# A macaron block of two feed-forwards and a retention layer on one core: the third feed-forward by seven block products of W2 instead of eight, with the block sums of W2 built one feed-forward earlier

## The reference

```
x = x + 0.5 * ffn(layernorm(x))
x = x + attention(layernorm(x))
x = x + 0.5 * ffn(layernorm(x))

ffn(h)       = fwht(silu(h W1^T) * (h W3^T)) W2^T      # W1, W3: 2048 x 512, W2: 512 x 2048
attention(h) = chunked linear attention with per-head decay, 16 heads of 32, 4 chunks of 128,
               ternary-quantised qkv and output weights, RMS norms in front and behind
```

## Time and profile before

| | us |
|---|---|
| median of 3 runs | 2299.95 (2299.61 to 2300.54) |
| profiled execution | 2298.74 |
| its span, first to last instruction | 2297.0 |
| TensorE busy | 2274.4 (99%) |
| VectorE busy | 1518.2 (66%) |
| ScalarE busy | 925.9 (40%) |
| GpSimd busy | 219.4 (10%) |
| share of the 16 DMA engines, main queue | 46.6% |

### The profile page before, as it was taken

How to read it: one execution, slowest core, us unless ns; L and a number is a source line. 1 busy time by engine, 2 the same in 40 slices (tenths; PEclk the granted TensorE clock), 3 DMA queues, 4 the chain that set the end, 5 groups by cost and what they waited for, 6 DMA issues and landing times. The chain is left out here.

```text
span 2297.0 us, 48771 instructions
## 1 busy us (share of the span) xinstructions
PE 2274.4 (99%) x19551; PEld 1775.0 (77%) x19551; DVE 1518.2 (66%) x3430; ACT 925.9 (40%) x1897; POOL 219.4 (10%) x206
## 2 busy tenths in 40 slices
PE   9999999999999999999999999999999999999998
PEld 5444444687888788888888888788878887888887
DVE  7677456676777667767666677676667766666544
ACT  7646134434343433344334344433344344334322
POOL 0290014110000000000000000000010000000000
PEclk9999999999999999999999999999999999999999
DMA  9866533344444533555255345632546326442422
GB/s 243 224 160 180 161 100 86 121 121 126 130 118 127 147 92 119 134 140 139 74 154 140 91 129 140 154 93 81 165 118 148 97 77 173 102 118 78 117 92 67
DMA packets 349698, 291.57 MB, mean 127 GB/s; under 512 B 253600, under 2 KB 278432, under 8 KB 346656
## 3 DMA queue, kind: packets, MB, share of 16 engines
q1 hardware_dynamic: 349040, 287.66, 46.6%
q10 hardware_dynamic: 432, 0.79, 0.1%
HBM read 173.02 MB, written 59.77 MB: 101 GB/s over the span
## 5 line engine op out<-in xcount | busy, mean ns | idle before, releaser
L1960 PE MATMUL d_bank<-w2t,work 128*128 128x256 f16 x2496 | 374.4, 272 | 2.4 <-DMA work<-w_dram 2.4
L1535 DVE SCALAR_TENSOR_TENSOR work<-l_bank,l_scale,work 128x256 f32<-128x256 f32 x416 | 181.7, 478 | 260.6 <-PE l_bank L1928 259.9
L1928 PE MATMUL g_bank<-work,w1t 128*128 128x256 f16 x2688 | 311.7, 272 | 1.8 <-ACT work L1172 1.8
L1928 PE MATMUL l_bank<-work,w3t 128*128 128x256 f16 x2688 | 311.7, 273 | 0.0
L1928 PEld LDWEIGHTS l_bank<-work,w3t 128*128 128x128 f16 x2688 | 261.7, 98 | 36.4
L1928 PEld LDWEIGHTS g_bank<-work,w1t 128*128 128x128 f16 x2688 | 259.9, 98 | 33.9 <-ACT work L1172 2.4
L1552 DVE TENSOR_TENSOR work<-work 128x256 f16<-128x256 f32 (+1 forms) x416 | 257.1, 618 | 33.3 <-ACT work L1184 32.8
L1182 ACT CAST work<-work 128x256 f16<-128x256 f32 x208 | 84.1, 404 | 470.3 <-DVE work L1540 466.4
L1960 PE MATMUL d_bank<-work 128*128 128x256 f16 x1872 | 272.5, 273 | 0.5 <-DVE work L1552 0.5
L1172 ACT ACTIVATE work<-g_bank,g_scale 128x256 f32<-128x256 f32 x416 | 173.6, 468 | 236.5 <-PE g_bank L1928 236.4
L1960 PEld LDWEIGHTS d_bank<-w2t,work 128*128 128x128 f16 x2496 | 240.6, 98 | 35.2 <-issue 2.9
(11 more groups left out here) (282 smaller groups left out, 2915.7 us busy)
## 6 DMA issues: line engine op xcount, KB each, us to landing
work<-w_dram SPq DMA_DIRECT2D x208, 384.0 KB, 3.4
work<-parts_dram SPq DMA_DIRECT2D x192, 128.0 KB, 3.4
x_dram<-work SPq DMA_DIRECT2D x16, 1024.0 KB, 4.6
work<-x_dram SPq DMA_DIRECT2D x24, 512.0 KB, 4.6
parts_dram<-q_parts SPq DMA_DIRECT2D x32, 256.0 KB, 2.1
parts_dram<-k_parts SPq DMA_DIRECT2D x32, 256.0 KB, 2.4
norm_dram<-cent SPq DMA_DIRECT2D x32, 256.0 KB, 2.3
w2t<-in_L_ffn_W_dram SPq DMA_DIRECT2D x31, 256.0 KB, 3.5
```

The lines of the kernel that those rows point to most:

```text
L1535: nc.vector.scalar_tensor_tensor(out=tokens, in0=l_bank[:, HALF * e:HALF * (e + 1)], scalar=l_scale[:, tile:tile + 1], in1=second_gate if ...
L1928: ins = nc.tensor.matmul(dst[:, HALF * e:HALF * (e + 1)], wt[:, wp, k, P * tile:P * (tile + 1)], f.x[:, s_half, xp, k, :], start=(k == 0 a ...
L1960: ins = nc.tensor.matmul(bank_m[:, cols], combos[:, q % 2, hp, combo, :], weights[:, wp, :], start=(p == 0 and opens and hp == wp), stop=( ...
```

## The change

`FAST` becomes 2, so that n = 2 is done by seven block products too; the plain `feed_forward` falls away, and the fast one takes its name. The step `w2sums` is split in two: GpSimd's part keeps the name, the casts, low parts and the store become `w2halve`. Both are now hung on slots: `w2sums` p at slot 3p - 14 (-14, -11, -8, -5, -2, 1, 4, 7), `w2halve` p at slot 3p - 11 (-11, -8, -5, -2, 1, 4, 7, 10). The first four of the `w2halve` steps thus stand among the `down` steps of n = 1, the rest in n = 2. The f32 sums and one single staging buffer `w2_staged` lie in `yt`, the operand of n = 3; ACT waits for the store of pair p - 1 before it writes the staging buffer for p. TensorE waits for the sums pair by pair in the first half of n = 2, and no longer for all of them. The layer norm `("ffn1", 3)` moves from slot 19 to slot 12, since n = 2 now writes x1 half-way.

```diff
-    FAST = 3
+    FAST = 2
...
-        w2_sums = at["hid_f32"].rearrange("p (i d) -> p i d", i=4)
+        w2_sums = at["yt"][:, 0:4 * HALF].rearrange("p (i d) -> p i d", i=4)
+        w2_staged = at["yt"][:, 4 * HALF:7 * HALF].bitcast(F16).rearrange("p (a i d) -> p a i d", a=2, i=3)
...
+            for p in range(PAIRS):
+                add(slots, max(3 * p - 14, -HT), [("w2sums", p)])
+                add(slots, 3 * p - 11, [("w2halve", p)])
...
-            for at, b in ((19, 3), (109, 4), (253, 5), (353, 6), (470, 7)):
+            for at, b in ((12, 3), (109, 4), (253, 5), (353, 6), (470, 7)):
...
-        for n in range(2, FAST):
+        for n in range(FAST, 2 * B):
             STEPS += feed_forward(n, SLOTS)
-        for n in range(FAST, 2 * B):
-            STEPS += fast_feed_forward(n, SLOTS)
...
-                elif step == "w2sums":
+                elif step == "w2halve":
                     sp.wait_ge(w2_sum_lo, 2 * (arg + 1))
-                    sp.dma_start(w2_dram[arg], streamed[:, arg % 2]).then_inc(w2_stored[arg % 2], 16)
+                    sp.dma_start(w2_dram[arg], w2_staged).then_inc(w2_stored[arg % 2], 16)
...
-                elif step == "w2sums":
+                elif step == "w2halve":
                     p = arg
                     act.wait_ge(w2_differences, p + 1)
-                    if p >= 2:
-                        act.wait_ge(w2_stored[p % 2], 16 * (p // 2))
                     nc.scalar.copy(w2t[:, p, 0, HALF:D], w2_sums[:, 0]).then_inc(w2_sum_hi, 1)
-                    nc.scalar.copy(streamed[:, p % 2, 0], w2_sums[:, 1:4]).then_inc(w2_sum_hi, 1)
+                    if p:
+                        act.wait_ge(w2_stored[(p - 1) % 2], 16 * ((p - 1) // 2 + 1))
+                    nc.scalar.copy(w2_staged[:, 0], w2_sums[:, 1:4]).then_inc(w2_sum_hi, 1)
...
                     pe.wait_ge(w2_streamed[q % 2], 16 * (q // 2 + 1))
+                    if n == FAST and s_half == 0:
+                        pe.wait_ge(w2_sum_lo, 2 * (p + 1))
                     if p == 0:
-                        pe.wait_ge(w2_sum_lo, 2 * PAIRS)
                         pe.wait_ge(res_done, TT * FAST)
```

37 lines of the change are left out of this document (7 added, 30 removed).

## The result

| | before | after |
|---|---|---|
| median | 2300.13 (2298.31 to 2301.49, 15 runs) | 2304.74 (2303.25 to 2308.90, 15 runs) |
| ratio to before | | 1.0022, 95% interval 1.0015 to 1.0029 |
| profiled execution | 2298.74 | 2304.92 |
| span | 2297.0 | 2303.2 |
| mean granted clock | 1.000 | 0.997 |

What follows compares the result with a forecast made beforehand. TensorE was taken as the bound, busy for 2274.4 of 2297.0 us. The terms -3.7 - 4.0 + 1.8 + 0.6 + 0.2 summed to -5.1 us, giving a median of 2294.8 us, range 2291.8 to 2299.5.

Steps and rivals of the forecast that it cites:

- Step 1: In n = 2, fewer matmul columns, with pairs of 7.53 us: 3.7 us less.
- Step 2: In n = 2, TensorE's three stalls at 358 to 365 us go: 4.0 us less.
- rival (c): The n = 2 stalls move instead of going, 3 us return: sum -2.1, 2297.8 us; chance 0.13.
- Step 3: In n = 1, reloads come late behind the store of pair 1: 1.8 us more, bounds 0 and 5.
- Rival (a): In n = 1, norm operations collide with GpSimd's adds at the shared port; reloads cost 5.0: 2298.0 us, chance 0.17.
- Step 4: Start of n = 2: added DVE work delays v's second half, 0.6 us more, bounds 0 and 2.2.
- Step 5: Rest of n = 2: more DVE work per pair and sixteen new streams, 0.2 us more, bounds 0 and 2.
- The prediction's own test: The prediction counts as wrong if, among other signs, n = 2 as a whole is not shorter by 6 us or more.
- Rival (d): In n = 1, a store in SP's queue holds up reload 13; 8 us late gives 2302.8 us; chance 0.05.

Runs made afterwards that it cites:

- b_nosums: The kernel before the change, with the building of W2's block sums left out and plain pieces stored instead: 2295.37 us, ratio 0.9980.
- e_norm: The changed kernel with the layer norm of batch 3 at slot 16 instead of 12: 2302.02 us, ratio 1.0009.
- e_comb2: Changed kernel: v before k's transposes, pair 1's store behind reloads, batch 3's norm at 16, n = 2's store at 51, later sums re-slotted: 2295.18 us.
- e_early: The changed kernel with casts and low parts of pairs 0 and 4 to 7, and pair 1's adds, in earlier slots: 2305.89 us, ratio 1.0027.
- e_nosums: The changed kernel with the building of W2's block sums left out and plain pieces stored instead: 2298.27 us, ratio 0.9994.
- e_vfirst: The changed kernel with batch 0's v in front of the transposed k in slot 1: 2301.63 us, ratio 1.0008.
- e_plain_tuned: The changed kernel without W2's block sums, v in front of k's transposes, n = 2's result store at slot 51: 2291.81 us, ratio 0.9965.
- e_store: The changed kernel with only the store of n = 2's result moved to slot 51: 2303.03 us, ratio 1.0014.
- e_filler: The changed kernel with 12 unneeded matmuls of 512 columns in the wait between v's halves: 2305.60 us, ratio 1.0026.

## Why the prediction was wrong

**Step 1, fewer columns, was right.** A pair of n = 2 without attention work takes 424.56 - 417.03 = 7.53 us in the changed kernel:

```profile
417.03 2.78 PE L1904 MATMUL g_bank<-xt,w1t 128*128 128x256 f16 x24
...
424.56 0.67 PE L2009 MATMUL a_bank<-work 128*128 128x128 f16 x9
```

**Step 2 was right on the old stalls and wrong on what is late next.** No wait is left between 340 and 370 us, and `b_nosums` prices the old ones at 4.6 us by the medians and 4.1 by the traces. But a stall of the same kind came at 331 us, which is rival (c). I had ended `w2sums` 7 near 320 us by a period of 8.3 us a pair. (The prediction's own numbers give 265.5 + 6 x 8.3 = 315.3.) It ended at 329.63, because the casts and low parts of pairs 5 to 7 stand at fixed places in DVE's and ACT's order, three slots apart, and DVE reached them at 309.58, 321.08 and 330.95: 10 to 12 us a pair, set by the slots and not by the chain. GpSimd stood idle for 7.7, 7.5 and 5.1 us in front of pairs 5, 6 and 7, waiting for DVE. In size this is the largest miss of the sum: 3.4 us of idle time and 2.9 us of slow matmuls behind it, against 0. `e_norm` and `e_comb2` take the stall away in the two pieces that stood in front of the score, 1.2 us each.

**Step 3 had the right mechanism, and its size was off by 0.9 us.** After the change the chain runs as the prediction has it. First GpSimd's timeline, the adds and differences of `w2sums` 1:

```profile
259.51 3.06 POOL L962 TENSOR_TENSOR work<-w2t 128x512 f32<-128x512 f16 x2 [9.35 <-DVE work L1499]
262.65 1.05 POOL L964 TENSOR_TENSOR work<-work 128x256 f32<-128x256 f32 x1
...
265.72 1.05 POOL L967 TENSOR_TENSOR work<-work 128x256 f32<-128x256 f32 x1
```

DVE beside it, two row operations of the norm and the last low parts of pair 1:

```profile
260.11 1.46 DVE L1649 SCALAR_TENSOR_TENSOR cent<-work,mean,qnw_row 128x512 f32<-128x512 f32 x1
...
263.23 1.03 DVE L1649 SCALAR_TENSOR_TENSOR cent<-work,mean,qnw_row 128x512 f32<-128x512 f32 x1
...
267.98 0.96 DVE L1499 TENSOR_TENSOR work<-work 128x768 f16<-128x768 f32 x1 [0.31 <-ACT work L1135]
```

And SP's queue, the store of pair 1 and the three reloads behind it:

```profile
268.96 0.32 SPq L785 DMA_DIRECT2D w_dram<-work  x1
269.39 1.37 SPq L737 DMA_DIRECT2D work<-hid_dram  x3
```

`w2sums` 1 started at 259.51 (forecast 259.5), took 7.3 us (6.0), and the reloads went out at 269.39 (268.2), where before they went at 264.53. The wait in front of `down` 13 is 1.46 us (1.5); that these two agree is luck, since the reloads went out 1.2 us later than forecast and `down` 13 was itself held back by the wait in front of `down` 11. What I had priced at nothing is the shift of the norm's rows and of the reloads between their transposes: it costs the 0.91 us in front of `down` 11. `e_early`, with pair 0's casts ahead of the norm, has neither wait. Rival (a), by which every norm operation beside the adds collides, stood for a turn of 9.2 us. The Trainium skill, "SBUF — State Buffer", section "Who interferes with whom", states that rule. The trace agrees that there is a collision, in both directions (1.46 and 1.03 us for operations of 0.75, 1.05 for differences of 0.72), but the turn grew by 1.8 us, less than half of the 3.8 that five full collisions would make.

**Step 4 is the step that failed.** It was priced at 0.6 us and cost 2.8 us of idle time and 1.7 us of slow matmuls. I had listed the instructions in front of v's low parts, and then not added their durations. They are in one piece of DVE's timeline:

```profile
289.42 0.88 DVE L1511 SCALAR_TENSOR_TENSOR work<-l_bank,l_scale,work 128x256 f32<-128x256 f32 x2 [3.56 <-PE l_bank L1904]
...
291.26 1.40 DVE L1492 SCALAR_TENSOR_TENSOR work<-d_bank,ffn_unscale,xin 128x512 f32<-128x512 f32 x2
292.58 0.41 DVE L1528 TENSOR_TENSOR work<-work 128x256 f16<-128x256 f32 x1
292.91 0.55 DVE L1707 TENSOR_TENSOR kT<-k_turned_parts 128x384 f32<-128x384 f16 x1
```

Before, the step of `lin` took DVE from 286.44 to 287.11, 0.67 us, and then came the transposed k; now `hlin`, two `resid` and `hlow` take 292.91 - 289.42 = 3.49 us ahead of it. From there to v's low parts, over the transposed k and ACT's cast and copies, it is 2.30 us in both kernels (287.11 to 289.41, and 292.91 to 295.21). The difference, 2.82, is the growth of the wait from 0.29 to 3.13 (2.84). There was no slack to set against it, since TensorE had already waited there before. `e_nosums` shows that the sums have no part in it, `e_vfirst` and `e_plain_tuned` that the order of v and k decides 2.3 us of it.

**Step 5 had the resource right and missed its place.** The streams of n = 2 cost nothing. The one of n = 3 came late by 1.5 us, behind the store of n = 2's result, which is issued 13.8 us after the start of n = 3 where it was 10.3 (455.34 - 441.57, and 444.64 - 434.29); it went with the store (`e_store`).

**A term was missing: the clock.** Nowhere did the sum allow for what follows a stall of 3 us. In the profiled execution it was 1.7 + 1.65 + 1.28 = 4.6 us of the 6.2 us by which the two spans differ; in that of the kernel before the clock never fell. `e_filler` and `e_store` show the part of v without it.

How much of it is in the median can be estimated, since each run's mean granted clock is on record. Of 80 runs of the kernel before, made beside the experiments, the 12 at 1.000 have a median of 2298.1 us, the 53 at 0.999 one of 2299.9 and the 15 at 0.998 one of 2301.4. So the forecast, which took 1.2 us from the profiled execution to the median, took it from an execution without a fall. The mean over the 80 runs is 0.99896, over the 15 of the changed kernel 0.99753; the difference, 0.0014 of 2300 us, is 3.3 us, of the 4.6 between the medians. Taken at the same 0.998 the two kernels are 2.9 us apart (2304.4 against 2301.4), which leaves 1.7 us for the clock. So by these two estimates the clock makes 1.7 to 3.3 us of the loss, and the waits the rest.

The prediction's own test, that n = 2 be shorter by 6 us or more, failed: from the first gate of n = 2 to that of n = 3 it is 157.6 us, against 153.2 before. Rival (d), the only one on the slower side, named the wrong place: SP's queue cost 1.4 us, and DVE at v and at the score 6 us of idle time. That the measured time came out on rival (d)'s side was not for its reason.

## What to carry to other kernels

Where a change puts work in front of an engine's instruction for which TensorE already waits a little, there is no slack, and here the whole of the added durations was paid (2.82 us on DVE, 2.84 us on TensorE): write out that row of instructions and add it up. A wait that the profile puts down to one engine is checked against what the waiting instruction needs: in `e_filler` the engine named had been done for 4.6 us. Steps hung on slots went here at the pace of the slots and not of their own chain, so where the last of them ends is read from the slots. A forecast of a median should start from runs at the same granted clock as the median's. A schedule that loses can hold a form that wins: take away the disputed work on both sides first (here 2298.27 against 2295.37), then its new waits one by one; four moved steps turned +4.6 us into -3.2, and other slots for the later sums turned that into -4.7.
